# Thirty-two unused products in the warm-up of the first attention of a four-layer kernel

## The reference, cut to what matters

```python
x = x + tanh(g_xattn[0]) * L0_xattn(layernorm(x), ctx_768, ...)   # the stage changed here
x = x + tanh(g_ffn[0])   * L0_ffn(layernorm(x), ...)
...                                                                # three more layers

# L0_xattn: 16 heads of 8
q = x @ q_w.T + q_b
v = cross @ v_w.T + v_b
scores = einsum('bhld,bhcd->bhlc', q, v) / sqrt(8)    # v takes the place of k
out = softmax(scores) @ v @ o_w.T + o_b
```

## Time and profile before

| what | value |
|---|---|
| median of three runs | 2090.84 us (2085.31, 2090.84, 2097.4) |
| the profiled execution's own time | 2093.74 us |
| its span, first to last instruction | 2091.8 us |
| mean granted clock of TensorE | 0.896 of full |
| PE busy | 1767.5 us, 84% of the span |
| DVE / ACT / POOL busy | 64% / 61% / 56% |

### The profile page before, as it was taken

The page is one execution under the profiler, slowest core; times in us unless marked ns, Lnnn a source line. Parts: engine busy times, 40 slices in busy tenths (PEclk is TensorE's granted clock), DMA queues, the critical chain, the costliest instruction groups (busy, mean ns, idle before and its releaser), DMA issues. The chain is left out here.

```text
span 2091.8 us, 55280 instructions
## 1 busy us (share of the span) xinstructions
PE 1767.5 (84%) x22172; PEld 1233.1 (59%) x22173; DVE 1331.4 (64%) x2607; ACT 1271.2 (61%) x1629; POOL 1163.5 (56%) x1083
## 2 busy tenths in 40 slices
PE   3999549999739499999999999999727739999788
PEld 1444328888637246666666666666516628888645
DVE  4578678888744465556555655555325548888765
ACT  2377338888534157777777777777515528888543
POOL 4312216666433357777777777777552336876434
PEclk7699669999869689999999999999857859999789
DMA  7322000000230200000000000000221020000000
GB/s 177 50 32 33 15 1 3 3 3 3 62 112 19 59 9 11 12 13 11 11 11 14 11 11 11 13 12 8 62 77 46 30 78 3 3 3 3 1 6 16
DMA packets 96847, 55.20 MB, mean 26 GB/s; under 512 B 43389, under 2 KB 90824, under 8 KB 96502
## 3 DMA queue, kind: packets, MB, share of 16 engines
q1 hardware_dynamic: 92052, 44.32, 8.9%
q0 software_dynamic: 3584, 6.36, 0.9%
q10 hardware_dynamic: 962, 0.99, 0.2%
HBM read 30.16 MB, written 13.75 MB: 21 GB/s over the span
## 5 line engine op out<-in xcount | busy, mean ns | idle before, releaser
L1518 POOL TENSOR_TENSOR aw_p_lo<-aw_p,aw_p_hi 128x512 f16<-128x512 f32 x512 | 576.1, 1156 | 190.6 <-issue 169.1
L1534 DVE TENSOR_REDUCE aw_max_part<-ps 128x1 f32<-128x512 f32 x512 | 351.2, 690 | 288.9 <-PE ps L1340 284.1
L1470 ACT ACTIVATE aw_p<-ps 128x1024 f32<-128x1024 f32 x256 | 259.8, 1015 | 205.6 <-PE ps L1371 203.4
L954 POOL TENSOR_TENSOR ap_p_lo<-ap_p,ap_p_hi 128x512 f16<-128x512 f32 x256 | 290.7, 1156 | 166.2 <-issue 156.9
L1385 PE MATMUL ps<-ctx_hi_lo,aw_p_hi 128*128 128x97 f16 x2048 | 288.9, 206 | 2.5 <-POOL aw_p_lo L1518 2.5
L1387 PE MATMUL ps<-ctx_hi_lo,aw_p_hi 128*128 128x96 f16 x2048 | 288.0, 207 | 0.0
L1389 PE MATMUL ps<-ctx_hi_lo,aw_p_lo 128*128 128x97 f16 x2048 | 287.4, 204 | 0.0
L1477 ACT ACTIVATE aw_p_hi<-aw_p 128x1024 f16<-128x1024 f32 x256 | 270.6, 1057 | 8.1
L1387 PEld LDWEIGHTS ps<-ctx_hi_lo,aw_p_hi 128*128 128x128 f16 x2048 | 197.9, 97 | 25.2
L1385 PEld LDWEIGHTS ps<-ctx_hi_lo,aw_p_hi 128*128 128x128 f16 x2048 | 196.4, 96 | 12.1 <-POOL aw_p_lo L1518 4.7
L1389 PEld LDWEIGHTS ps<-ctx_hi_lo,aw_p_lo 128*128 128x128 f16 x2048 | 201.9, 99 | 0.0
(11 more groups left out here) (509 smaller groups left out, 4997.1 us busy)
## 6 DMA issues: line engine op xcount, KB each, us to landing
sf_weights_raw<-in_L_w SPq DMA_DIRECT2D x24, 256.0 KB, 4.4
slot_scratch<-x_normT SPq DMA_DIRECT2D x16, 260.0 KB, 8.6
sf_fetched<-slot_scratch SPq DMA_DIRECT2D x16, 260.0 KB, 3.3
sf_weights_raw<-in_L_w SPq DMA_DIRECT2D x8, 512.0 KB
x_norm<-result_scratch SPq DMA_DIRECT2D x8, 256.0 KB, 4.1
aw_queries<-aw_queries SPq DMA_DIRECT2D x32, 64.0 KB, 2.0
aw_queries<-aw_q_lo SPq DMA_DIRECT2D x32, 64.0 KB, 2.1
aw_queries<-aw_queries SPq DMA_DIRECT2D x32, 36.0 KB
```

The costliest lines, as they stand in the source:

```text
L954: nc.gpsimd.tensor_tensor(p_lo[:, i % 2, h, :], p[:, i % 2, h, :], p_hi[:, i % 2, h, :], ALU.subtract).then_inc(lo_done, 1)
L1470: nc.scalar.activation(p[:, n % 2, :].rearrange("p (b q) -> p b q", b=2), s, ACT.Exp, scale=1.0 / QS).then_inc(exp_done, 1)
L1518: nc.gpsimd.tensor_tensor(p_lo[:, n % 4, cols], p[:, n % 2, cols], p_hi[:, n % 4, cols], ALU.subtract).then_inc(lo_done, 1)
L1534: nc.vector.tensor_reduce(mpart[:, b % 2, k:k + 1], ps[:, max_bank(b, k), :], AX.X, ALU.max).then_inc(m_done, 1)
```

## The change

A helper `filler(r)` issues four products of 97 rows by 128 columns of weights on 512 moving columns, from operands that lie in SBUF already, into bank 6. Nothing reads the result, and the first real product into that bank starts a new sum. It is called ahead of everything else in each quarter of steps -3 and -2. In quarter 0 it first waits for both value semaphores, in both steps.

```diff
+                def filler(r):
+                    if r == 0:
+                        pe.wait_ge(v_even, NT // 2)
+                        pe.wait_ge(v_odd, NT // 2)
+                    for _ in range(4):
+                        nc.tensor.matmul(ps[:, UB, :], M.ct_hi[:, 0:P], M.w0v_hi[:], start=True, stop=True)
+
...
                 for b in range(-3, NB + 1):
                     for r in range(4):
+                        if b < -1:
+                            filler(r)
                         n = 4 * b + r
```

## The result

| | before | after |
|---|---|---|
| median, 20 runs each | 2087.78 us | 2081.47 us |
| lowest and highest | 2077.28, 2097.4 | 2071.86, 2086.32 |
| ratio, 95% interval | | 0.9967 (0.9951 to 0.9983) |
| profiled span, mean clock | 2091.8 us, 0.896 | 2073.0 us, 0.914 |

The change makes the program 0.33% faster, some 7 us (3.5 to 10). I had said 1.1 us. The measured 2081.47 us lie under the range that I gave; that the difference stays within 0.5% held. The spans of the two profiled executions differ by 19 us, far more than the kernels do: one execution is a poor witness here.

The account below looks back on a forecast made before the run. TensorE (PE) at half clock was taken as the bound in parts of the first attention. Terms +0.44 - 0.48 - 1.1 made -1.1 us, from the 2090.84 us median to 2089.7; range 2083 to 2098.

Parts of the forecast that it names:

- Step -3, +3.47: Warm-up step -3: all 16 fillers stand ahead of query(0) behind the 1.51 us idle gap, uncovered, costing +3.47 us.
- Step -2, +2.60 - 5.63: Warm-up step -2: fillers in quarters 1 to 3 cost +2.60 us; its own work at full clock saves 5.63.
- Step -1, -0.48 - 1.1: Step -1, without fillers: first max_scores save 0.48 us and full_query(0) 1.1 at full clock, then the clock falls.
- the sum: Forecast total over the first attention's steps: +0.44 - 0.48 - 1.1 = -1.1 us.
- The step that failed: Blocks 0 and on: steps run as before until the clock returns at the same place, between 108 and 109: 0.
- Rival 1: First attention: the clock never falls, steps take 7.56 us from the start; -8.5 us in all, 2082.4 us; chance 0.12.
- Rival 2: Clock falls at the 1.51 us gap despite fillers: about +5, 2095.8 us, or +11.7 without a return; chance 0.15.
- Rival 3: Clock holds through step -2, falls in step -1, returns a step later: +2.3 us, 2093.1 us; chance 0.18.
- the forecast's pattern: Block steps after the fall in step -1: diagonal products spaced as before, 9.23, 12.07 and 8.72 us; chance 0.55.

Follow-up runs that it names:

- cut kernels: Kernels before and with the change, or with other filler placements, ended behind the first attention with its unprojected result written out; means 229.8 us before, 224.7 changed.

## Why the prediction was wrong

**Step -3, +3.47: right.** 3.45 us in the trace, and 3.4 (2.0 to either side) between the cut kernels with and without it.

**Step -2, +2.60 - 5.63: right, a little better than said.** `fold` takes 0.97 us at full clock (71.03 to 72.00), half of what it took, not 1.18; the four fillers in front of `max_scores` take 0.96 (72.00 to 72.96 in the trace), not 0.87, so a quarter is 2.46 us for my 2.53. Counted from the end of the gap, the first `max_scores` of step -1 starts after 16.00 us (65.44 to 81.44) and did after 15.85: +0.15, where I had +0.44.

**Step -1, -0.48 - 1.1, and the fall in it: right.** These terms end with `full_query(0)`, where the next `max_scores` start. In the kernel before they start at 85.89:

```profile
85.89 1.03 PE L631 MATMUL ps<-at_keys,at_q_hi 16*128 16x256 f16 x4
```

That is 19.06 us behind the gap's end (66.83). After the change it is 17.73 us (65.44 to 83.17): -1.3 for the -1.1 of the sum. The clock fell in the first, second and fourth profile at 85.4 to 86.3, in the third at 81.8, and in the two cut ones not at all.

**The step that failed:** "With the clock fallen in step -1 the steps run as before until it comes back. Before, it came back between 108 and 109. I set this at the same place: 0." The return is not at a place. In the changed kernel it came at 93.1, 93.1, 109.1 and 95.6, in the one before at 108.8, 93.7, 89.4 and 94.6. What the change buys is a difference of means over such draws, and I took both from one execution, whose stage was the longest of the six that were profiled of the kernel before, cut ones included. In place of the 0 the cut kernels show some 4 us less: the gain up to the end of the stage is 5.1 us, with 3.8 to either side, where the sum had 1.1. By that margin the size of the term is barely known; that the return moves is seen in every trace.

The predicted time missed by 8.2 us (2089.7 against 2081.47). The change accounts for 5.2 of them (6.3 between the medians, for 1.1). The other 3.1 are the starting point, a median of three runs (2090.84) that 20 runs put at 2087.78. The range was too narrow below for both reasons.

**Rival 1** (no fall) is what two of six profiles of the change show, both of the cut kernel; their stage time is 53.2, 10 us under that of my trace, where I had 8.5 as the ceiling. I gave it 0.12. **Rival 2** (a fall at the gap in spite of the fillers) was seen in none of the six. **Rival 3** (a late return) came near once: in the third profile the steps lie 9.23, 12.07 and 9.82 us apart, which is between the forecast's pattern (8.72 for the last) and the rival's (12.07).

**What stays open.** The traces don't show the gain of the change. Over six profiles each, cut ones included, half clock in the stage is 21.6 us before and 8.5 after on average, but the stage time is 55.6 and 56.3: the traces bear out that the clock is held, and that the fillers' own time eats what this gives, about as the sum had it. The gain is in the means of the timed executions, most likely through bad draws that no trace caught. With fillers in step -2 alone the two stage times, whole and cut, are 52.1 and 49.7 us, under both averages. The later stages were not looked at: from the next stage's first product to the end the kernel before took 1856 to 1866 us in four profiles and the changed one 1857 to 1865, which neither shows nor excludes that some of the gain is made there. Nor is it shown why the fillers of step -3 alone bring nothing in the whole program, and nothing more when step -2 has its own.

## What to carry to other kernels

When the clock of TensorE falls at a short idle gap, the cost is not the gap but the stretch of work behind it that runs at half clock without bringing it back; here products of 97 rows there bought it back, and as many of 16 rows cost their time and bought nothing. Put them where the engine waits anyway: those on the path cost their full time, and the cut kernel was fastest without the 16 that stood there. Where the clock's return differs from run to run, read it from several executions, and time the stage by itself before trusting a sum made on one trace.

## What the runs showed of the hardware

The record of the granted clock can leave a stretch at half clock out. In the opening PE has nothing to do for some 20 us. For that stretch the record of the changed kernel's first profile says full clock, that of its third half:

```profile
21.00:40.00 19.00, 0.00 (x0) 0.00 (x0) 5.97 (x16) 3.21 (x6) 0.10 (x1) 1.00 0.77 212
```

```profile
21.00:40.00 19.00, 0.00 (x0) 0.00 (x0) 5.97 (x16) 3.20 (x6) 0.38 (x3) 0.50 0.74 214
```

But the first products behind it, here of the first profile, lie 0.43 us apart, as at half clock, until 44.9:

```profile
41.03 0.63 PE L585 MATMUL ps<-ctxT_hi,w0k_lo 97*128 97x512 f16 x1
41.45 0.63 PE L586 MATMUL ps<-ctxT_lo,w0k_hi 96*128 96x512 f16 x1
...
45.52 0.38 PE L584 MATMUL ps<-ctxT_hi,w0k_hi 97*128 97x512 f16 x1
45.73 0.38 PE L585 MATMUL ps<-ctxT_hi,w0k_lo 97*128 97x512 f16 x1
```

So it is in all 20 profiles: the products behind the idle time start at half clock and change to 0.22 us between 43 and 48. The record has this in 8 of the 20. In the first attention the spacing of the wide products and the record agree in all of them, so the readings above hold; where a clock matters, look at both.

The Trainium skill, TensorE: Matmul & The Clock Gate, section Part 1: The HAM clock gate, gives the half rate as the state of an idle engine. The spacing of the products agrees with it in all 20 profiles.

And a busy PE can stay at half clock: 12.00 of 12.00 us busy at 0.50 with 16-row fillers, against 11.18 of 12.00 at 1.00 with those of 97 rows.
